# Four pieces of layer 1's attention in another order on TensorE, and two on VectorE

## The reference

```python
w = xp.reshape(B, nW, WIN, H, hd)                      # WIN = 64, nW = 8 windows
attn = softmax(einsum('bnqhd,bnkhd->bnhqk', w, w) * scale)
local = einsum('bnhqk,bnkhd->bnqhd', attn, w)
comp = conv(x, conv_w, stride 4)[:, :G] + conv_b       # G = 64 compressed tokens
gt = concatenate([comp, global_memory], axis=1)        # 128 keys for all tokens
ga = softmax(einsum('bshd,bghd->bhsg', xm, gt) * scale)
glob = einsum('bhsg,bghd->bshd', ga, gt)
mix = sigmoid(concatenate([local, glob]) @ gate_w + gate_b)
out = (mix * local + (1 - mix) * glob) @ out_w + out_b
...
gout = x @ Wgate + bgate                               # the router of the experts
topv, topi = top_k(gout, 2)
```

## Time and profile before

| what | us |
|---|---|
| median of 3 timed runs | 1380.31 (1378.35 to 1384.34) |
| the profiled execution, its own time | 1372.89 |
| its span, first to last instruction | 1371.1 |
| TensorE busy over the span | 1123.0 (82%) |
| VectorE busy | 800.4 (58%) |
| GpSimd busy | 583.9 (43%) |
| ScalarE busy | 502.0 (37%) |
| TensorE's mean granted clock | 0.901 of full |

### The profile page before, as it was taken

How to read it: one execution, slowest core, us unless ns; L and a number is a source line. 1 busy time by engine, 2 the same in 40 slices (tenths; PEclk the granted TensorE clock), 3 DMA queues, 4 the chain that set the end, 5 groups by cost and what they waited for, 6 DMA issues and landing times.

```text
span 1371.1 us, 20897 instructions
## 1 busy us (share of the span) xinstructions
PE 1123.0 (82%) x6836; PEld 670.0 (49%) x6836; DVE 800.4 (58%) x2040; ACT 502.0 (37%) x1137; POOL 583.9 (43%) x708
## 2 busy tenths in 40 slices
PE   2778787876649994699999999999942899999990
PEld 1356554555325663345556556456531455555550
DVE  2488888987422223435647767756554455565565
ACT  1334444433315553032442443343410344434440
POOL 0257777777524554503234455452353123222321
PEclk9999999998679997579999999999955999999995
DMA  7676776563145222101101112001112511111106
GB/s 295 146 184 158 171 180 151 131 167 86 39 117 192 79 78 71 59 9 36 37 26 48 31 49 63 27 28 30 29 43 69 173 32 35 36 37 35 36 20 192
DMA packets 96047, 117.28 MB, mean 86 GB/s; under 512 B 11176, under 2 KB 81320, under 8 KB 92984
## 3 DMA queue, kind: packets, MB, share of 16 engines
q1 hardware_dynamic: 86984, 97.46, 26.7%
q0 software_dynamic: 8704, 17.97, 4.0%
q10 hardware_dynamic: 256, 0.53, 0.2%
HBM read 85.35 MB, written 32.17 MB: 86 GB/s over the span
## 4 chain that ended last, share of the span: by engine, by line
PE 49%; DVE 5%; issue 3%; POOL 1%; DMA 1%; SPq 1%; ACT 1%; POOLq 0%; DVEq 0%; ACTq 0%
PE bank L1976 9%; PE bank L2218 4%; PE bank L1962 4%; PE bank L2161 4%; PE bank L2115 3%; PE bank L1986 3%; PE bank L2168 3%; PE bank L2198 2%; PE bank L2127 2%; PE bank L1970 2%; PE bank L2200 2%; PE bank L2187 2%; PE bank L2232 1%; PE bank L2183 1%; PE bank L1746 1%
## 5 line engine op out<-in xcount | busy, mean ns | idle before, releaser
L1163 POOL DMA_INDIRECT slots<-pay,slot x128 | 129.4, 1011 | 82.5 <-issue 71.6
L1178 POOL DMA_INDIRECT y<-region,xin x80 | 76.8, 960 | 190.9 <-ACT region L1540 170.6
L1976 PE MATMUL bank<-wgl,rows 128*128 x288 | 138.5, 604 | 5.8 <-ACT rows L1523 5.8
L979 DVE TENSOR_REDUCE rows<-bank 128x4 f32<-128x512 f32 x128 | 79.4, 683 | 74.4 <-PE bank L2115 74.1
L1523 ACT ACTIVATE rows<-bank 128x256 f32<-128x256 f32 x216 | 80.8, 382 | 101.4 <-PE bank L1970 100.3
L1178 POOL DMA_INDIRECT y<-hh,region x64 | 61.2, 957 | 119.9 <-ACT hh L1540 105.3
L734 DVE TENSOR_TENSOR rows<-bank,w0uv 128x512 f32<-128x512 f32 x72 | 49.7, 691 | 95.5 <-PE bank L1976 86.8
L1659 ACT ACTIVATE w0uv<-bank 128x512 f32<-128x512 f32 x128 | 66.1, 603 | 88.7 <-PE bank L2168 88.7
L726 DVE TENSOR_TENSOR rows<-region,bank 128x256 f32<-128x256 f32 x72 | 30.3, 421 | 113.4 <-ACT region L1528 113.4
L1970 PEld LDWEIGHTS bank<-consts,rows 128*128 128x128 f32 x432 | 57.9, 142 | 73.8 <-issue 50.6
L1201 POOL TENSOR_TENSOR region<-region 128x512 f32<-128x512 f32 x64 | 81.4, 1285 | 13.9 <-DVE region L866 12.8
(11 more groups left out here) (320 smaller groups left out, 2412.1 us busy)
## 6 DMA issues: line engine op xcount, KB each, us to landing
region<-vrdram SPq DMA_DIRECT2D x16, 1024.0 KB, 9.4
region<-vrdram SPq DMA_DIRECT2D x32, 512.0 KB, 8.7
xin<-slots SPq DMA_DIRECT2D x80, 65.0 KB
region<-slots SPq DMA_DIRECT2D x64, 65.0 KB
wgl<-in_wgl SPq DMA_DIRECT2D x1, 4096.0 KB, 13.0
rows<-y SPq DMA_DIRECT2D x8, 512.0 KB, 4.3
wgl<-y SPq DMA_DIRECT2D x8, 512.0 KB, 7.5
xres<-x SPq DMA_DIRECT2D x12, 256.0 KB, 2.3
```

What stands on the lines that cost most here:

```text
L979: V.tensor_reduce(maxg[:, t, g * QD:g * QD + HG], bank[g].rearrange("p (h k) -> p h k", h=HG), axis=AX, op=ALU.max).then_inc(S["c_mx"], 1)
L1163: p.indirect_dma_start(io["slots"], bass.IndirectOffsetOnAxis(ap=slot_of(l, b)[:, k, t:t + 1], axis=0), pay_of(l, b)[:, k, t, :], None).th ...
L1178: p.indirect_dma_start(io["y"], bass.IndirectOffsetOnAxis(ap=xins[par][:, h, k, P + 1:P + 2].bitcast(U32), axis=0), bYs[par][:, h, k, :], ...
L1976: ins = M(bank[k][:, :], bT[:, k, tile(c)], wgl[:, bass.ds(ex_of[h][k], 1), c, :].squeeze(1), start=c == 0, stop=c == FC - 1)
```

## The change

In TensorE's step, behind `less_global(i, 0)`, the pieces stand in another order. Before: `compress`, `score_local(i, 0)`, `attend_local(b, 1, 1)`, `route`, `again_global(i, 1)`, `less_global(i, 1)`. Now: `attend_local(b, 1, 1)`, `score_local(i, 0)`, `again_global(i, 1)`, `compress`, `less_global(i, 1)`, `route`. On VectorE `norm_local(b, 1, 1)` stands ahead of `max_local(i, 0)`, no longer behind it. ScalarE and GpSimd keep their lists; no instruction is added or taken away, and no wait is changed.

```diff
@@ VectorE's step
             def step(i):
                 a, b, c, d, f = i + 1, i - 1, i - 2, i - 3, i + 2
+                if ok(b):
+                    norm_local(b, 1, 1)
                 if ok(i):
                     max_local(i, 0)
-                if ok(b):
-                    norm_local(b, 1, 1)
                 if ok(a):
                     global_keys(a, a % 2)
@@ TensorE's step
                 if ok(i):
                     less_global(i, 0)
+                if ok(b):
+                    attend_local(b, 1, 1)
+                if ok(i):
+                    score_local(i, p, 0)
+                    again_global(i, p, 1)
                 if ok(a):
                     compress(a, a % 2)
                 if ok(i):
-                    score_local(i, p, 0)
-                if ok(b):
-                    attend_local(b, 1, 1)
+                    less_global(i, 1)
                 if ok(d):
                     route(d)
                 if ok(i):
-                    again_global(i, p, 1)
-                    less_global(i, 1)
                     attend_global(i, 0)
                     score_local(i, p, 1)
```

## The result

The changed kernel takes 1424.14 us, median of 4 runs (1419.49 to 1427.81), against 1379.33 for the kernel before in the same comparison: a ratio of 1.0324 (95% interval 1.0274 to 1.0373), slower by about 45 us. The forecast was slower by 11. The profiled execution has 1424.19, a span of 1422.4 and a granted clock of 0.860, where before had 1372.89, 1371.1 and 0.901: between these two the difference is 51.3.

What follows compares the result with a forecast made beforehand. TensorE's list was taken to bound layer 1's attention. Waits of +10.2 and a clock term of +1.1 gave 11.3, say +11, on the timed median: 1391 us, range 1382 to 1400.

Steps and rivals of the forecast that it cites:

- the chain of waits: Layer 1's attention: the new order exposes again_global's last bank, convolution, less_global and route behind the maxima; +10.2 us at full clock.
- the clock after: Half-clock stretches on TensorE in the new order: +4.5 at the changed place, -3.4 elsewhere in the attention, together +1.1 us.
- The pacing bank by bank: again_global directly behind the scores goes at VectorE's pace; its last bank's product starts 0.14 behind the maxima and takes 1.07.
- the maxima that don't move: attend_local ahead of score_local: ScalarE's exponentials cover it, so scores end and maxima start as before; cost and gain 0.
- VectorE's edit at 0: norm_local ahead of max_local: its 0.9 us fits into VectorE's idle 5.07 before the maxima; cost 0.
- rival 2: again_global's last bank overlaps with the convolution or counts as a quarter: +4.6 us, 1385; chance 0.15.
- Rival 3: The new hole before again_global lowers TensorE's clock in every step: +22 us, 1402; chance 0.10.
- Rivals 1 and 4: Half-clock stretches in the attention go: +1.7 us, 1382, chance 0.14; or the timed runs lose more, -5.7, 1374.6, chance 0.05.
- the other place: Late in steps, around again_local, untouched by the change: five of seven steps at half clock, two fewer forecast, -3.4 us.

Runs made afterwards that it cites:

- e3: Changed kernel plus one dense product of 512 columns, result unread, between score_local and again_global in each of eight steps; 1390.05 us, ratio 1.0061.
- h2: Changed kernel with the convolution ahead of attend_local and route between the scores and again_global; 1403.59 us, ratio 1.0130.
- h1: Changed kernel with the convolution alone moved back, between the scores and again_global; 1391.74 us, ratio 1.0074.
- e4: Changed kernel with convolution and route both between the scores and again_global; 1376.17 us, ratio 0.9968 against the kernel before.
- f1: Kernel before plus one dense product of 512 columns, result unread, between attend_local and route; 1386.41 us, ratio 1.0031.
- f3: Changed kernel plus four thin products of 8 columns, results unread, between the scores and again_global; 1422.99 us, ratio 1.0286.
- g3: Changed kernel plus one dense product of 512 columns between the convolution and less_global, the hole left open; 1424.18 us, ratio 1.0321.

## Why the prediction was wrong

The direction and the chain of waits were right. The step that failed is the term "the clock after": taken at +1.1, it came to about +35 (45 less the 10.2 of the chain; e3 gave 34 of them back).

**The chain of waits: single numbers right to a tenth.** At full clock behind the maxima, as in e3, the trace shows them. The forecast for a step with `route` was +2.32 from `less_global` to `attend_global`; e3 measures 11.43 against 9.14, +2.29. Without the convolution (step 7) it was +1.0, and e3 has 10.12 against 9.14. The hole before `again_global` was to be 0.9 in each step, put down to L986, and is 0.92 in all eight. The waits of the changed kernel from 600 to 1040 list (us in total, times, longest):

```profile
PE bank L2161 <- DVE wam L986: 7.5, 8, 1.0
```

Seven of these eight are the holes of steps 1 to 7; the eighth, 1.03, stands ahead of `again_global` of round 2 in step 0. Step 0's own hole (587.38) lies ahead of the window. The kernel before has that one too (TensorE in its step 0):

```profile
590.13 3.01 PE L2161 MATMUL bank<-hT,rows 32*128 32x512 f32 x6 [0.92 <-DVE wam L986]
```

So the change opens seven new holes, not eight. The one of step 0 lies in a part at half clock in both kernels (0.50 up to 594.5 in before), and so couldn't show beforehand whether a hole lowers a clock that is at full.

The pacing bank by bank, the maxima that don't move, VectorE's edit at 0 beside TensorE's: all as written. From the end of the maxima to `attend_global` e3 has 856.12 - 851.85 = 4.27, where 4.29 was forecast. And the convolution follows the end of the maxima by 852.96 - 851.85 = 1.11, so rival 2, that the last bank's product would cost less, is out. Summed over the eight steps, from `less_global` to `attend_global`, e3 has 90.8 against 80.5, or +10.3, next to the 10.2 of the sum. That the two agree so well is partly luck: 1.3 of it is a half-clock stretch of e3 in step 1, and step 0 has +0.5 where +2.0 was forecast. Up to `max_T_local` only +5.5 is left: from `attend_global` to there steps 3 to 7 of e3 are each 0.3 to 0.5 shorter (the prediction had counted 0.27 in steps 5 and 6), and step 0 is 2.7 shorter as a whole.

**The clock: the step that failed.** "The clock after" was +4.5 for the changed place, within bounds of 0 and +12, and -3.4 for the other. The upper bound took all eight steps at 1.5, the mean of three stretches behind `route` in steps 3 to 5. Two things were wrong in it.

First, the price of one. In the kernel before the clock was back after one stretch of 3.4. In the new order convolution and `route` stand right where the clock has just fallen, spread over twice their time, and three stretches follow each other. Within the changed kernel, steps 1 and 2, without `route`, are at half clock for 6.8 behind the hole, and steps 4 to 7 for 10.2; with the 6.8 of h2 this speaks for the thin work as what prolongs it. It isn't shown: step 7 of h1, in the same order as step 7 of the changed kernel, has 6.8 and not 10.2. In step 5, `less_global` to `turn_out` (L2232) is 896.75 - 877.66 = 19.1; in e3 at full clock it is 859.03 - 844.69 = 14.3. The clock costs 4.8 there, not 1.5.

Second, how often. I took three of eight steps, from the share that before had. Of the seven steps with a new hole six are hit: only step 3 has none behind it, and why isn't shown (a spell of 20.4 us ends 4.8 us ahead of its hole). In all it is 54.4 us at half clock in this place in steps 1 to 7, where before had 10.2. I had written that an empty stretch can be no better than a thin one, and then still counted it as one that is hit in three cases of eight.

Over eight steps the part from `less_global` to `max_T_local` grew by 35.3 us (162.9 to 198.3; e3 has 168.4, so some 30 of it are the clock's) and the rest between, which the change doesn't touch, by 15.0 (224.7 to 239.7), mostly in two spells of 17 and 20 us. I had forecast -3.4 for the latter, by two fewer stretches. These are numbers of one profiled execution each. Of the latter the runs explain little: spells of 20 us also come in e4's profiled execution (three) and in f1's (one). Whether the new order brings them on more often isn't shown.

**The rivals.** Rival 3, the hole lowering the clock in every step, came nearest, at a chance of 0.10 and a price of +22 instead of +45: it had six steps of the seven right and the length of the spell too short. And it isn't the idle time that does it, as f3 shows, but the little work there. Rivals 1 and 4, in which the clock pays, had the sign wrong: with the thin products apart the clock fell more often, not less.

The Trainium skill's page "TensorE: Matmul & The Clock Gate" says in its Part 1, on the clock gate, that the granted ratio is set by how busy TensorE has been recently. f3 against e3 puts a finer point on it: both are busy for 3.40 of 3.40 us around the hole, and only the dense one keeps the clock (1.00 behind it, against 0.50). The traces agree with the page if "busy" is read as work done, and not if it is read as the profile's busy time.

## What to carry to other kernels

Before thin work is taken out of the time in which an engine waits for another, look at both things that it does there: it covers the wait, and it is part of what keeps TensorE's clock up. Don't price a fall of the clock by the single stretch that the old order shows: here that was 1.5 us in a step, and in the new order, with thin pieces behind the hole, it was 4.8. Don't count on dense work behind the hole to end it either: in g3 the spells were shorter in some steps and longer in step 5. And if a change opens a hole of even 0.9 us next to thin products, try it once with a useless dense product in the hole: if the kernel gets faster by doing more, the clock is the cause.

## What the runs showed of the hardware that was not expected

Holes of 0.92 us, one in each of eight steps, were enough to cost 34 us by the lower clock. One dense fp32 product of 512 columns in the hole (1.05 us) took that back. One of 128 columns, which left 0.50 of the hole open, and four of 8 columns, which filled it for 1.00 us, took back nothing; the convolution, four of 64 columns (1.11 us), took back 32, of which about 8 are the shorter chain of waits. Once the clock had fallen, stretches at half clock came in a row, up to three behind the hole of the changed kernel (10.2 us) and six in the other place (20.4 us at 0.50).
